# Cross attention: bias of the exponential on GpSimd, scaling of the finished tile on ScalarE, query placing in two parts

## What is computed

```python
q = (x @ Wq + bq).reshape(1, B * N, H, hd)          # H = 16 heads of hd = 16
kv = (cond @ Wkv + bkv).reshape(1, -1, 2, H, hd)    # 1024 queries on 1024 keys
k, v = (kv[:, :, 0], kv[:, :, 1])
scale = 1.0 / np.sqrt(hd).astype(np.float32)
...
q = _fq_sym(q, axis=-1)                             # rounded to 127 levels with a scale per row
k = _fq_sym(k, axis=-1)
v = _fq_sym(v, axis=2)                              # a scale per column
attn = jnp.einsum('bhqd,bhkd->bhqk', q, k)
attn = jax.nn.softmax(attn.astype(jnp.float32), axis=-1)
attn = _fq_unsigned(attn, axis=-1)                  # rounded to 255 levels of the row's maximum
out = jnp.einsum('bhqk,bhkd->bhqd', attn, v)
out = jnp.transpose(out, (0, 2, 1, 3)).reshape(B, N, C)
return out @ Wp + bp
```

## Time and profile before

| what | before |
|---|---|
| time, median of 3 runs | 1125.81 us (1124.47 to 1127.17) |
| the profiled execution | 1125.34 us, its span 1123.6 us |
| mean granted TensorE clock | 0.824 |
| busy: PE, DVE, ACT, POOL | 831.1, 786.2, 487.9, 545.6 us |
| first and last row maximum of the 128 units | start at 736.32 and 928.08 us |

### The profile page before, as it was taken

How to read it: one execution, slowest core, us unless ns; L and a number is a source line. 1 busy time by engine, 2 the same in 40 slices (tenths; PEclk the granted TensorE clock), 3 DMA queues, 4 the chain that set the end, 5 groups by cost and what they waited for, 6 DMA issues and landing times. The chain is left out here.

```text
span 1123.6 us, 12980 instructions
## 1 busy us (share of the span) xinstructions
PE 831.1 (74%) x4458; PEld 542.4 (48%) x4481; DVE 786.2 (70%) x1317; ACT 487.9 (43%) x695; POOL 545.6 (49%) x394
## 2 busy tenths in 40 slices
PE   5987989767677776785879567767667676789990
PEld 2553754356566665664753255623333334445650
DVE  4756366399999999999833576689999993423332
ACT  2312122354545546546430333588888882112210
POOL 2207000489779789797720122257777762310005
PEclk9978989978887886887889889868776766689995
DMA  4010030000000000000035000659999993151113
GB/s 154 1 39 36 1 119 1 0 1 1 1 1 0 1 1 1 1 1 1 0 103 200 0 1 1 242 103 177 186 175 170 169 169 58 47 178 38 57 54 115
DMA packets 155582, 73.05 MB, mean 65 GB/s; under 512 B 138827, under 2 KB 151565, under 8 KB 154446
## 3 DMA queue, kind: packets, MB, share of 16 engines
q1 hardware_dynamic: 153982, 68.03, 26.5%
q0 software_dynamic: 1536, 4.20, 1.2%
HBM read 27.11 MB, written 11.53 MB: 34 GB/s over the span
## 5 line engine op out<-in xcount | busy, mean ns | idle before, releaser
L726 POOL TENSOR_TENSOR r_pairs<-r_side_exp 128x1035 f32<-128x1035 f32 x128 | 248.4, 1972 | 8.9 <-DVE r_w L891 7.8
L781 PE MATMUL r_head_sum<-ident,r_w 128*128 128x128 f32 (+1 forms) x1024 | 154.7, 316 | 85.4 <-ACT r_w L809 62.7
L809 ACT ACTIVATE r_w<-r_w,r_scale 128x1001 f32<-128x1001 f32 (+1 forms) x128 | 144.6, 1140 | 162.7 <-DVE r_w L891 141.0
L781 PEld LDWEIGHTS r_head_sum<-ident,r_w 128*128 128x128 f32 (+1 forms) x1024 | 141.3, 168 | 106.8 <-ACT r_w L809 80.3
L1596 ACT ACTIVATE c_probs<-c_scores,c_bias,c_q_scale 128x1024 int16<-128x1024 f32 x128 | 154.2, 1205 | 30.2 <-DVE c_bias L1609 21.4
L1607 DVE TENSOR_REDUCE c_neg_max<-c_scores 128x1 f32<-128x1024 f32 x128 | 155.6, 1215 | 6.5 <-PE c_scores L1547 6.3
L1534 POOL CAST kv_parts<-c_probs 128x1024 bf16<-128x1024 int16 x128 | 132.4, 1041 | 54.7 <-ACT c_probs L1596 53.7
L883 DVE SCALAR_TENSOR_TENSOR r_chosen<-r_pairs,r_kept,r_z 128x1024 f32<-128x1024 f32 (+1 forms) x112 | 141.4, 1277 | 13.1 <-ACT r_sims L793 4.3
L1547 PE MATMUL c_scores<-c_kT,c_placed 128*128 128x512 bf16 x233 | 99.5, 513 | 56.8 <-ACT c_probs L1596 52.2
L891 DVE TENSOR_TENSOR r_w<-r_pairs,r_chosen 128x1024 f32<-128x1024 f32 (+1 forms) x112 | 135.0, 1206 | 0.0
L757 PE MATMUL r_head_sum<-r_up,r_wT 128*128 128x256 f32 (+1 forms) x256 | 73.5, 457 | 13.5 <-ACT r_wT L820 13.5
(11 more groups left out here) (275 smaller groups left out, 1436.0 us busy)
## 6 DMA issues: line engine op xcount, KB each, us to landing
sorted_rows<-b_zeros SPq DMA_DIRECT2D x1, 4096.0 KB, 22.2
e_row<-sorted_rows SPq DMA_DIRECT2D x8, 512.0 KB, 7.3
expert_rows<-e_made SPq DMA_DIRECT2D x8, 512.0 KB, 2.9
en_w<-in_w SPq DMA_DIRECT2D x1, 2992.0 KB, 11.6
ew_w<-in_w SPq DMA_DIRECT2D x1, 2992.0 KB, 13.0
ew_w_near<-in_w_near SPq DMA_DIRECT2D x1, 2176.0 KB, 20.0
r_up<-in_up SPq DMA_DIRECT2D x1, 2048.0 KB, 10.2
c_pT<-kv_parts SPq DMA_TRANSPOSE x128, 3.3
```

The costliest lines, as they stand in the source:

```text
L726: nc.gpsimd.tensor_tensor(pairs[:, v % MADE, :].rearrange("p (a b) -> p a b", b=KEYS), a.broadcast_to([P, ROWS, KEYS]), b.broadcast_to([P, ...
L781: last = nc.tensor.matmul(head_sum[0:m, b // 4, (b % 4) * P:(b % 4 + 1) * P], w[:, v % RING, b * P:b * P + m], ident[:, :], start=(h == 0 ...
L809: nc.scalar.activation(w[:, v % RING, 0:COLS[f]], w[:, v % RING, 0:COLS[f]], ACT.Silu, scale=scale[:, t % 2, h:h + 1]).then_inc(silu_done, 1)
```

## The change

The bias of the exponential is now computed on GpSimd by `shift(u)`: for units 0 and 1 ahead of the loop, and for unit u + 2 behind the cast of unit u. VectorE signals its maximum by a new semaphore, `max_ready`, and does no more for a unit. `scale_values` stands on ScalarE, behind the exponential of head 14 (for the last tile behind the last exponential). `place_queries` places one of the two heads of each pair in a call; one call stands at head 4, the other at head 6, and each waits for the cast and the bias ahead of it.

```diff
@@ -1351,7 +1351,8 @@
                     at = slice(own * P // 2, (own + 1) * P // 2)
                     nc.gpsimd.memset(s.placed[at, half, :, 1 - own, :], 0.0).then_inc(s.placed_zeroed, 1)
             pool.wait_ge(turned_copied, KV + 1)
-            place_queries(nc, s, 0)
+            for own in range(2):
+                place_queries(nc, s, 0, own)
             pool.wait_ge(s.placed_zeroed, 4)
             pool.wait_ge(s.q_placed, 2)
 
@@ -1453,11 +1454,10 @@
                                       whole[:, :, 0:1, :].broadcast_to([P, QT * HEADS_C, PARTS - 2, HD_C])).then_inc(q_whole, 1)
 
 
-def place_queries(nc, s, t):
-
-    for own in range(2):
-        at = slice(own * P // 2, (own + 1) * P // 2)
-        nc.gpsimd.tensor_copy(s.placed[at, t % 2, :, own, :], s.qT[at, :, t * P:(t + 1) * P]).then_inc(s.q_placed, 1)
+def place_queries(nc, s, t, own):
+
+    at = slice(own * P // 2, (own + 1) * P // 2)
+    nc.gpsimd.tensor_copy(s.placed[at, t % 2, :, own, :], s.qT[at, :, t * P:(t + 1) * P]).then_inc(s.q_placed, 1)
 
 
 def attend(nc, sh, s):
@@ -1475,7 +1475,8 @@
         MIX_LAG = 8
         HELD = 2
         PAIR_C = 2 * HD_C
-        PLACE_AT = 4
+        PLACE_AT = (4, 6)
+        SHIFTED = 2
         TURN_AT, SCALE_AT, PROJECT_AT, ADD_AT = 4, 6, 9, 11
         LOG_LEVELS = float(np.log(LEVELS_P))
         UNITS_C = NT * HEADS_C
@@ -1489,7 +1490,8 @@
         scores = ps("scores", [P, SCORED, 2, HALF])
         mixed = ps("mixed", [P, 1, HALF])
         tail = ps("tail", [P, 1, HALF])
-        scored, bias_ready, exp_done, rounded_ready = sem("scored"), sem("bias_ready"), sem("exp_done"), sem("rounded_ready")
+        scored, max_ready, bias_ready = sem("scored"), sem("max_ready"), sem("bias_ready")
+        exp_done, rounded_ready = sem("exp_done"), sem("rounded_ready")
         turned = [sem("turned%d" % n) for n in range(IN_FLIGHT)]
         mixed_ready, o_ready, oT_ready, oT_copied, out_ready, out_added = (
             sem("mixed_ready"), sem("o_ready"), sem("oT_ready"), sem("oT_copied"), sem("out_ready"), sem("out_added"))
@@ -1520,18 +1522,30 @@
 
         @block.gpsimd
         def _(pool):
+            def shift(u):
+                t, h = divmod(u, HEADS_C)
+                pool.wait_ge(max_ready, u + 1)
+                nc.gpsimd.tensor_scalar(bias[:, t, h:h + 1], neg_max[:, t, h:h + 1], s.q_scale[:, t, h:h + 1], LOG_LEVELS,
+                                        ALU.mult, ALU.add).then_inc(bias_ready, 1)
+
+            for u in range(SHIFTED):
+                shift(u)
             for u in range(UNITS_C):
                 t, h = divmod(u, HEADS_C)
-                if h == PLACE_AT and t + 1 < NT:
-                    pool.wait_ge(rounded_ready, u)
+                if h in PLACE_AT and t + 1 < NT:
                     if t >= 1:
                         pool.wait_ge(scored, HEADS_C * t)
-                    place_queries(nc, s, t + 1)
-                    pool.wait_ge(q_placed, 2 * (t + 2))
+                    own = PLACE_AT.index(h)
+                    pool.wait_ge(rounded_ready, u)
+                    pool.wait_ge(bias_ready, u + SHIFTED)
+                    place_queries(nc, s, t + 1, own)
+                    pool.wait_ge(q_placed, 2 * (t + 1) + own + 1)
                 pool.wait_ge(exp_done, u + 1)
                 if u >= ROUNDED:
                     pool.wait_ge(turned[(u - ROUNDED) % IN_FLIGHT], turned_count(u - ROUNDED))
                 nc.gpsimd.tensor_copy(rounded[:, u % ROUNDED, :], probs[:, u % RING, :]).then_inc(rounded_ready, 1)
+                if u + SHIFTED < UNITS_C:
+                    shift(u + SHIFTED)
             norm_pool(nc, pool, sh.ln, sh.ln.norms + 1)
 
         @block.tensor
@@ -1588,6 +1602,14 @@
 
         @block.scalar
         def _(act):
+            def scale_values(t):
+                act.wait_ge(oT_ready, t + 1)
+                if t >= 1:
+                    act.wait_ge(out_ready, t)
+                for c in range(DC):
+                    last = nc.scalar.activation(oT[:, c, :], tail[:, 0, c * P:(c + 1) * P], ACT.Copy, scale=s.v_scale[:, c:c + 1])
+                last.then_inc(oT_copied, 1)
+
             for u in range(UNITS_C):
                 t, h = divmod(u, HEADS_C)
                 act.wait_ge(bias_ready, u + 1)
@@ -1596,6 +1618,9 @@
                 nc.scalar.activation(probs[:, u % RING, :], scores[:, u % SCORED, :, :].rearrange("p a b -> p (a b)"), ACT.Exp,
                                      bias=bias[:, t, h:h + 1], scale=s.q_scale[:, t, h:h + 1],
                                      accum_out=row_sum[:, t, h:h + 1]).then_inc(exp_done, 1)
+                if u >= MIX_LAG + HEADS_C and (u - MIX_LAG) % HEADS_C == SCALE_AT:
+                    scale_values((u - MIX_LAG) // HEADS_C - 1)
+            scale_values(NT - 1)
 
         @block.vector
         def _(dve):
@@ -1604,10 +1629,8 @@
             def row_max(u):
                 t, h = divmod(u, HEADS_C)
                 dve.wait_ge(scored, u + 1)
-                chain.step(nc.vector.tensor_reduce(neg_max[:, t, h:h + 1], scores[:, u % SCORED, :, :].rearrange("p a b -> p (a b)"),
-                                                   AX.X, ALU.max, negate=True))
-                nc.vector.tensor_scalar(bias[:, t, h:h + 1], neg_max[:, t, h:h + 1], s.q_scale[:, t, h:h + 1], LOG_LEVELS,
-                                        ALU.mult, ALU.add).then_inc(bias_ready, 1)
+                nc.vector.tensor_reduce(neg_max[:, t, h:h + 1], scores[:, u % SCORED, :, :].rearrange("p a b -> p (a b)"),
+                                        AX.X, ALU.max, negate=True).then_inc(max_ready, 1)
 
             def normalise(t):
                 dve.wait_ge(exp_done, HEADS_C * (t + 1))
@@ -1623,14 +1646,6 @@
                         ALU.mult)
                 last.then_inc(o_ready, 1)
 
-            def scale_values(t):
-                dve.wait_ge(oT_ready, t + 1)
-                if t >= 1:
-                    dve.wait_ge(out_ready, t)
-                for c in range(DC):
-                    last = nc.vector.tensor_scalar(oT[:, c, :], tail[:, 0, c * P:(c + 1) * P], s.v_scale[:, c:c + 1], None, ALU.mult)
-                last.then_inc(oT_copied, 1)
-
             def residual(t):
                 dve.wait_ge(out_ready, t + 1)
                 nc.vector.tensor_tensor(x[:, t, :], x[:, t, :], tail[:, 0, 0:D], ALU.add).then_inc(out_added, 1)
@@ -1643,13 +1658,10 @@
                     t, h = divmod(u - MIX_LAG, HEADS_C)
                     if h == 0:
                         normalise(t - 1)
-                    if h == SCALE_AT:
-                        scale_values(t - 1)
                     if h == ADD_AT:
                         residual(t - 1)
             residual(NT - 2)
             normalise(NT - 1)
-            scale_values(NT - 1)
             residual(NT - 1)
 
 
```

## The result

The changed kernel takes 1142.29 us (median of 20 runs, 1135.21 to 1154.77), the kernel before, timed beside it, 1125.17 (20 runs, 1120.62 to 1136.55). The ratio is 1.0139 [1.0112, 1.0165]: 15.6 us slower by the ratio, 17 by the medians. I had said 1128.5 with a range of 1119 to 1136. It did get slower, as forecast, but by five times the 3 us, and outside the range.

What follows compares the result with a forecast made beforehand. VectorE was taken to set the pace before, a loop through GpSimd after. From 1125.34 us, -6.3 + 14.4 + 7.9 + 3.0 - 16.0 = +3.0 gave 1128.3, stated as 1128.5, range 1119 to 1136.

Steps and rivals of the forecast that it cites:

- the term -16.0: VectorE between reductions: normalising, scaling, residual, statistics and score waits, 16.0 us of the stage before, forecast to vanish.
- The length of the bias: New bias instruction on GpSimd: forecast 0.27 us, the middle of 0.184 and 0.354.
- the second rival: Bias on GpSimd: every small operand read pays, bias 0.354 us, a unit 1.372, total 1133.8 us; chance 0.2.
- The steady unit: Each cross-attention unit of layer 1: 1.33 us instead of 1.38, so 126 units gain 6.3 us.
- the loop: Through GpSimd over two units, exponential, cast, next bias, exponential of u+2: 2.39 us plus the bias, 1.33 a unit.
- the placing: Query copies on GpSimd at heads 4 and 6: 2.06 us a tile, 7 tiles, +14.4 us.
- the tile's end: Scaling on ScalarE, projection and residual delay the next tile's first heads: 1.32 us a tile, 6 tiles, +7.9 us.
- the first: Rival: bias on GpSimd is short and ScalarE's 1.29 us sets the pace, 1122.9 or 1120.1 us; chance 0.2.
- the third: Rival: steady unit gets no shorter because ScalarE needs 1.38 us itself, total 1131.5 us; chance 0.1.
- The fourth rival: The extras hide and SP's transposes, 1.37 us each, are the bound, total 1118.5 us; chance 0.05.
- The low clock: TensorE at the output projection: projection 1.07 us longer, score 0.43, so 1.5 in two tiles, +3.0 us.
- The chain: Head 14's exponential through scaling, projection, scores, maxima, residual and bias to the next tile's head 4 exponential: 9.30 us.

## Why the prediction was right or wrong

**What bounds the kernel before** was read rightly: VectorE. With the bias and the scaling off it, it is idle for 47.0 - 6.5 = 40.5 us more (14.6 of that is the longer stage; I had forecast idle time of some 25, not 47.0), and the term -16.0 for its other work is borne out: the longer stage is accounted for below with nothing of it left.

**The length of the bias** was right by luck, 0.267 against 0.27. I took the middle between paying for all and for no reads, and counted three small operands. It has two; the logarithm is in the instruction. 0.099 + 2 x 0.085 = 0.269 is the upper end, rightly counted, and the scale as a number took 0.075 off: that read does pay (the other wasn't taken away in any run). So what the second rival said of reads fits, and its 0.354 came of the third operand. The Trainium skill (GPSIMD Engine Reference, section 7, Performance pitfalls for Q7 kernels) has about 102 cycles for a small read command that doesn't pipeline with the one before. By the prediction's estimate that is 0.085, against 0.075 measured here.

**The steady unit** is the step that failed. I wrote "cast to the next GpSimd instruction 0.99, since five casts in a row took 4.98", and let the bias end where the next cast begins. By that, GpSimd's queue was 0.99 + 0.27 = 1.26, shorter than the loop's 1.33, and I didn't give it a sum of its own. Measured are 1.129 for the first and 0.06 on top of the bias for the second: 1.457, longer than the loop. 126 x (1.457 - 1.38) = +9.7 stands where I had -6.3. That is 16 us, the whole miss (12.4 by the sums) and more. That the side came out right is owed to the terms for the placing and the tile's end: of the steady unit, where the loss arose, I had forecast a gain. The rows had the warning: in the earlier trace rows two copies, each 1.03 long in after's row above, took 2.14, so they stood 0.06 apart with no wait between them, and the first cast, which does wait for them, came 0.06 later. I used both figures side by side and took the better one for a pair that I had never seen. None of the rivals had it either: the second is the same loop with another length, the first and third let ScalarE set the pace, the fourth SP, and none says that GpSimd's own queue is the bound.

**The placing**: 14.4 forecast, 7 x (8.22 - 5.83) = 16.7 measured. Each copy lies open in the queue as I had said, and splitting it gives nothing. The bias's hand-overs around it are larger, the same error again.

**The tile's end**: 7.9 + 3.0 forecast, 5.0 measured in six tiles (0.36, 1.34, 0.44, 1.99, 0.44, 0.44; the 1.34 and the 1.99 are those with a low clock at the projection). The low clock is some 2.4 of it, near the 3.0; the rest is 2.6 where I had 7.9. The chain was right even so: from the exponential of head 14 to that of the next tile's head 4 I had 9.30, and undisturbed tiles took 9.18 or 9.19. But six steady units are 8.74 at 1.457, and were 7.98 at my 1.33, so this is once more the steady unit. (ScalarE can follow faster than I said, exponentials 1.20 to 1.22 apart and not 1.29; the end of the accumulator read isn't its floor.)

By these steps the sum is +9.7 + 16.7 + 5.0 - 16.0 = +15.4, the same as from exponential to exponential.

**SP** was no bound in after: its transposes were issued at most 1.2 us behind the cast's end, where in before the largest lag was 3.6. **The fourth rival** is refuted with that, **the first** by the bias's length, and **the third** by exponentials 1.20 and 1.22 apart on the same ScalarE.
